# Third attention's reciprocals in long units, its normalisation two additions later, and five smaller moves in a four-layer network

## The reference

```
x += tanh(g0) * linear_attention(ln(x), ctx)      # L0_attn, feature maps Wqf, Wkf
x += tanh(g0') * ternary_ffn(ln(x))               # L0_ffn, 512 -> 2048 -> 512
x += tanh(g1) * masked_attention(ln(x), ctx)      # L1_attn, scores clipped to +-50, mask by key
x += tanh(g1') * product_key_experts(ln(x))       # L1_ffn, top 8 of 128 x 128 keys, 4 heads
x += tanh(g2) * attention_int8(ln(x), ctx)        # L2_attn, q and output weights and inputs quantised
x += tanh(g2') * moe(ln(x))                       # L2_ffn, 8 experts of 256, top 2
x += tanh(g3) * attention(ln(x), ctx)             # L3_attn
x += tanh(g3') * (shared + moe(ln(x)))            # L3_ffn, 8 experts of 352, top 2, shared 1408
attention: o = softmax(q k^T / sqrt(32)) v, per head, then o @ Wo + bo
```

## Time and profile before

| what | value |
| --- | --- |
| three runs | 3059.21, 3059.64, 3060.09 us; median 3059.64 |
| profiled execution, its own time | 3059.54 us |
| its span | 3057.8 us |
| mean granted TensorE clock | 0.932 of full speed |
| PE, DVE, ACT, POOL busy | 2632.1, 1753.8, 1196.7, 930.9 us |
| DMA | 333.52 MB |

### The profile page before, as it was taken

One profiled execution on the slowest core, in us unless ns is written; L12 is line 12 of the kernel. 1 busy time (PEld: TensorE's weight loads), 2 busy tenths in 40 slices (PEclk: granted clock), 3 DMA queues, 4 the chain that ended last, 5 costly groups with the idle time before them and its releaser, 6 DMA issues. The chain is left out here.

```text
span 3057.8 us, 36158 instructions
## 1 busy us (share of the span) xinstructions
PE 2632.1 (86%) x11447; PEld 1671.9 (55%) x11447; DVE 1753.8 (57%) x3263; ACT 1196.7 (39%) x2550; POOL 930.9 (30%) x434
## 2 busy tenths in 40 slices
PE   7998799788887679999959998738699998699898
PEld 3555487655434456656546553426476653477555
DVE  2444576467765989989377664512277773444221
ACT  0222222267743688788014555111125553222111
POOL 0222000066732110010015775033318982322122
PEclk9998899899988889999979999869899999799999
DMA  9663113665403410100063421074465430212722
GB/s 278 223 241 139 55 62 124 182 166 142 111 1 114 165 56 28 46 37 28 14 170 107 132 68 29 1 288 110 106 183 172 121 102 1 84 41 71 262 56 47
DMA packets 137548, 333.52 MB, mean 109 GB/s; under 512 B 18608, under 2 KB 21681, under 8 KB 133041
## 3 DMA queue, kind: packets, MB, share of 16 engines
q1 hardware_dynamic: 110192, 262.71, 27.7%
q0 software_dynamic: 12864, 29.06, 4.1%
q10 hardware_dynamic: 14336, 39.85, 3.9%
HBM read 237.24 MB, written 97.72 MB: 110 GB/s over the span
## 5 line engine op out<-in xcount | busy, mean ns | idle before, releaser
L1982 POOL TENSOR_TENSOR L_attn_total<-L_attn_total,L_attn_probs 128x2048 f32<-128x2048 f32 x103 | 471.8, 4581 | 31.6 <-ACT L_attn_probs L1910 22.1
L2016 DVE TENSOR_REDUCE L_attn_row_max<-L_attn_rows_ps 128x1 f32<-128x512 f32 x512 | 338.9, 684 | 149.6 <-PE L_attn_rows_ps L1776 145.5
L1910 ACT ACTIVATE L_attn_probs<-L_attn_s_ps 128x512 f32<-128x512 f32 x512 | 288.0, 601 | 269.1 <-PE L_attn_s_ps L1797 264.2
L521 PE MATMUL L_ffn_hidden<-L_ffn_x_high,L_ffn_up_high 128*128 128x512 f32 x688 | 295.9, 430 | 73.2 <-DVE L_ffn_routes L432 25.8
L1797 PE MATMUL L_attn_s_ps<-L_attn_q_stack,L_attn_k_stack 98*128 98x512 f32 (+1 forms) x768 | 311.7, 432 | 21.1 <-ACT L_attn_probs L1910 20.7
L398 ACT ACTIVATE L_ffn_sums<-sims 128x128 f32<-128x128 f32 x1024 | 314.5, 389 | 29.0 <-DVE L_ffn_routes L418 22.3
L521 PE MATMUL L_ffn_hidden<-L_ffn_x_low,L_ffn_up_high 128*128 128x512 f32 x688 | 272.8, 397 | 0.0
L1776 PE MATMUL L_attn_rows_ps<-L_attn_k_stack,L_attn_q_stack 96*128 96x512 f32 x512 | 223.1, 439 | 23.0 <-DVE L_attn_row_max L2016 17.1
L542 PE MATMUL L_ffn_y<-L_ffn_down_in,L_ffn_h 128*128 128x512 f32 x512 | 230.8, 596 | 1.9 <-DVE L_ffn_h L649 1.9
L1797 PEld LDWEIGHTS L_attn_s_ps<-L_attn_q_stack,L_attn_k_stack 98*128 98x128 f32 (+1 forms) x768 | 145.7, 194 | 158.1 <-ACT L_attn_probs L1910 73.3
L1910 ACT ACTIVATE L_attn_probs<-L_attn_s_ps,keep_mask 128x512 f32<-128x512 f32 x256 | 183.8, 783 | 82.8 <-DVE L_attn_s_ps L2028 82.4
(11 more groups left out here) (310 smaller groups left out, 4526.2 us busy)
## 6 DMA issues: line engine op xcount, KB each, us to landing
L_attn_k_stack<-k_parts SPq DMA_DIRECT2D x144, 256.0 KB, 4.8
L_attn_q_stack<-q_parts SPq DMA_DIRECT2D x72, 256.0 KB, 6.0
k_parts<-L_attn_stage SPq DMA_DIRECT2D x32, 512.0 KB, 2.8
L_attn_abs_in<-in_L_ffn_w SPq DMA_DIRECT2D x12, 1024.0 KB, 10.8
L_attn_kv_parts<-L_attn_part ACTq DMA_DIRECT2D x12, 1024.0 KB, 4.8
L_attn_ctx<-ctx_parts SPq DMA_DIRECT2D x24, 512.0 KB, 9.3
L_attn_wv<-L_attn_kv_parts SPq DMA_DIRECT2D x24, 512.0 KB, 7.1
q_parts<-L_attn_stage SPq DMA_DIRECT2D x24, 512.0 KB, 3.6
```

The lines of the kernel that those rows point to most:

```text
L521: last = nc.tensor.matmul(hidden_ps[0:m, b, side, :], w[:, i, e0:e0 + m], x_parts[xp][:, i, h * HALF:(h + 1) * HALF], start=(q == 0), stop ...
L1910: nc.scalar.activation(probs[:, g % P_SLOTS, h, :], s_ps[:, v % S_SLOTS, :], ACT.Exp, **kinds).then_inc(exp_done, 1)
L1982: nc.gpsimd.tensor_tensor(total[:], first, probs[:, g % P_SLOTS], ALU.add).then_inc(added, 1)
L2016: nc.vector.tensor_reduce(row_max[:, hq, i:i + 1], rows_ps[:, r % R_SLOTS, :], AX_X, ALU.max, negate=True).then_inc(max_done, 1)
```

## The change

Eight edits in one:

1. `linear_attention_block` loads wo and bo of L0 into its buffers for the value weights once these are used; the output block takes them from there.
2. The mask of L1 is loaded and made inside the attention block; `key_mask_block` goes.
3. `tile_stats.taken` is set again behind the guest work (`meanwhile`) in L1_ffn's block, so the L2 attention doesn't take the statistics a second time.
4. The L2 attention's opening order is another.
5. L2: the reciprocals are taken in eight parts of 64 columns at units 10, 10, 10, 14, 15, 16, 17, 17, where there were four of 128 at units 8 to 11.
6. L2: `normalise` stands behind addition kt = 5, not 3.
7. L2_ffn: two experts' weights are loaded in the norm block, and the other six in the routed block, once the scatter has landed.
8. The routed block no longer loads x back; the L3 attention does, at the head of SP's queue, and takes the statistics at S0 of its order, which is new too. In the other attentions S0 is first.

```diff
@@ def ffn_block(...), behind the call of meanwhile
+            env.tile_stats.taken = final
@@ def routed_block(...)
-    if not last:
-        env.tile_stats.begin(env)
             def _(sp):
+                sp.wait_ge(slots.scattered, 16 * PICKS * TILES)
                 sp.dma_start(sums.rearrange("(t p) d -> p t d", p=P), env.x[:]).then_inc(kept, 16)
                 load_weights(sp)
...
                 sp.wait_ge(summed, 16 * I)
-                if not last:
-                    for t in range(TILES):
-                        sp.dma_start(env.x[:, t, :], sums[t * P:(t + 1) * P, :]).then_inc(back[t], 16)
...
-                if not last:
-                    for t in range(TILES):
-                        dve.wait_ge(back[t], 16)
-                        env.tile_stats.take(env, dve, t)
-                    env.tile_stats.finish(dve)
@@ def streamed_attention_block(..., x_sums=None)
-    INVERT_AT = {u: part for part, u in enumerate((8, 9, 10, 11) if less_max_rows else (4, 6, 7, 8, 9, 10, 11, 12))}
-    INVERTED = SEQ // len(INVERT_AT)
-    NORM_KT = 3
+    invert_units = (10, 10, 10, 14, 15, 16, 17, 17) if made else (8, 9, 10, 11) if less_max_rows else (4, 6, 7, 8, 9, 10, 11, 12)
+    INVERT_PARTS = len(invert_units)
+    INVERT_AT = {u: [part for part, v in enumerate(invert_units) if v == u] for u in invert_units}
+    INVERTED = SEQ // INVERT_PARTS
+    NORM_KT = 5 if made else 3
...
     if made:
-        order = ("N0 X0 X1 N2 W0 W1 X2 X3 N4 Q00 V00 V01 X4 X5 W2 W3 N6 Q01 V02 V03 X6 X7 Q02 Q03 Q10 Q11 T0 Q12 Q13")
+        order = ("W0 W1 N0 N2 X0 X1 X2 X3 N4 Q00 W2 Q01 W3 V00 Q02 V01 N6 Q03 X4 X5 V02 X6 X7 V03 Q10 Q11 T0 Q12 Q13")
...
     else:
         order = ("N0 N1 K00 N2 N3 X0 X1 K01 N4 N5 X2 X3 W0 W1 V00 N6 N7 X4 X5 Q00 W2 W3 V01 X6 X7 Q01 K10 K11 "
                  "V02 V03 Q02 Q03 Q10 Q11 T0 Q12 Q13")
+    if x_sums is None:
+        order = "S0 " + order
+    else:
+        order = ("K00 K01 V00 V01 W0 W1 S0 N0 N1 V02 N2 N3 X0 X1 V03 N4 N5 X2 X3 Q00 W2 W3 N6 N7 X4 X5 Q01 X6 X7 K10 K11 "
+                 "Q02 Q03 Q10 Q11 T0 Q12 Q13")
...
+                if not less_max_rows:
+                    sp.dma_start(mask_raw[:], io["mask"]).then_inc(mask_loaded, 16)
+                if x_sums is not None:
+                    for t in range(TILES):
+                        sp.dma_start(env.x[:, t, :], x_sums[t * P:(t + 1) * P, :]).then_inc(x_back[t], 16)
                 parts.first_loads(env, sp)
...
+                def statistics():
+                    if not taken_before:
+                        for t in range(TILES):
+                            if x_sums is not None:
+                                dve.wait_ge(x_back[t], 16)
+                            nc.vector.bn_stats(stats[:, t, :], env.x[:, t, :]).then_inc(stats_done, 1)
...
@@ def linear_attention_block(..., wo_dram)
+                sp.wait_ge(v_done, CT)
+                sp.dma_start(wv[:], wo_dram).then_inc(env.wo_loaded, 16)
+                sp.dma_start(bv[:], io["bo"].partition_broadcast(P)).then_inc(env.wo_loaded, 16)
@@ def expert_layer(...), L2_ffn
+                    FIRST = 2
+                    def early(sp):
+                        slots.load_router(env, sp)
+                        for e in range(FIRST):
+                            load(sp, e)
+                    def rest(sp):
+                        for e in range(FIRST, EXPERTS):
+                            load(sp, e)
...
-                    routed_block(env, name, slots, (up_sb, down_sb), lambda sp: None, E, sums, last, ahead)
+                    routed_block(env, name, slots, (up_sb, down_sb), rest, E, sums, ahead)
```

More of the change, by code:

```diff
@@ L917, in _, with routed_block @@
                 dve.sem_inc(slots.placed, 1)
-def routed_block(env, name, slots, weights, load_weights, E, sums, last, ahead=None):
+def routed_block(env, name, slots, weights, load_weights, E, sums, ahead=None):
     nc = env.nc
@@ L1582, in streamed_attention_block @@
     env.wo_loaded = env.sem("wo_loaded")
+    x_back = [env.sem(f"x_back{t}") for t in range(TILES)] if x_sums is not None else []
     with ExitStack() as local:
@@ L1848, in _ @@
                         turn(0)
-                    elif item[0] not in "WN":
+                    elif item[0] not in "WNS":
                         for c in range(DC):
@@ L1936, in _ @@
                         high_turn(0)
+                if not less_max_rows:
+                    act.wait_ge(mask_step, 3)
                 for n in range(SETS):
@@ L2059, in quantised_pair @@
                     dve.sem_inc(xn_done, 2)
[L2061 to L2069, removed]
+                def statistics():
+                    if not taken_before:
+                        for t in range(TILES):
+                            if x_sums is not None:
+                                dve.wait_ge(x_back[t], 16)
+                            nc.vector.bn_stats(stats[:, t, :], env.x[:, t, :]).then_inc(stats_done, 1)
+                        for t in range(TILES):
+                            dve.wait_ge(stats_done, t + 1)
+                            nc.vector.bn_aggr(meanvar[:, t, :], stats[:, t, :]).then_inc(var_done, 1)
+                    dve.wait_ge(sd_done, 1)
+                    nc.vector.reciprocal(rstd[:], sd[:]).then_inc(rstd_done, 1)
+                    dve.wait_ge(rstd_done, 1)
+                if not less_max_rows:
+                    dve.wait_ge(mask_loaded, 16)
+                    keep = keep_mask[:, 1, :]
+                    nc.vector.tensor_scalar(keep, mask_raw[:], 0.5, None, ALU.is_gt).then_inc(mask_step, 1)
+                    dve.wait_ge(mask_step, 1)
+                    nc.vector.tensor_scalar(keep_mask[:, 0, :], keep, SCALE, None, ALU.mult).then_inc(mask_step, 1)
+                    dve.wait_ge(mask_step, 2)
+                    nc.vector.tensor_scalar(keep, keep, -1.0, BOUND, ALU.add, ALU.mult).then_inc(mask_step, 1)
                 for item in OPENING:
+                    if item[0] == "S":
+                        statistics()
                     if item[0] == "N":
@@ L2107, in _ @@
                         if u in INVERT_AT and n:
-                            invert(n - 1, INVERT_AT[u])
+                            for part in INVERT_AT[u]:
+                                invert(n - 1, part)
                         if less_max_rows and u == TURN_AT and n + 1 < SETS:
                             low_turn(n + 1)
-                for part in range(len(INVERT_AT)):
+                for part in range(INVERT_PARTS):
                     invert(SETS - 1, part)
@@ L2459, in _ @@
                 dve.wait_ge(abs_done, 3 * FG)
[L2462 to L2473, removed]
-                sp.dma_start(raw[:], io["mask"]).then_inc(loaded, 16)
-            @block.vector
-            def _(dve):
-                dve.wait_ge(loaded, 16)
-                nc.vector.tensor_scalar(keep[:], raw[:], 0.5, None, ALU.is_gt).then_inc(step, 1)
-                dve.wait_ge(step, 1)
-                nc.vector.tensor_scalar(keep_mask[:, 0, :], keep[:], 32 ** -0.5, None, ALU.mult).then_inc(step, 1)
-                nc.vector.tensor_scalar(keep_mask[:, 1, :], keep[:], -1.0, 50.0, ALU.add, ALU.mult).then_inc(step, 1)
-                dve.wait_ge(step, 3)
 def quantise_rows(nc, link, src, dst, top, tmp):
@@ L2521, in sb @@
             return local.enter_context(nc.sbuf_tensor(f"{name}_{n}", shape, dt))
-        if early:
+        if weights:
+            wo, bo = weights
+        elif early:
             wo, out_rows = env.out_weights[:, 0], env.out_weights[:, 1]
@@ L2758, in x_hat, with expert_layer @@
                 yield
-        def expert_layer(name, gate, shared, normalise, sums, last=False, ahead=None):
+        def expert_layer(name, gate, shared, normalise, sums, ahead=None):
             with sublayer() as local:
@@ L2886, in build @@
         if "L3_attn" in stages:
-            attention_layer("L3_attn", env.tanh_gates[:, 3:4], loads=loads3)
+            attention_layer("L3_attn", env.tanh_gates[:, 3:4], loads=loads3, x_sums=x_sums)
         between.close()
@@ L2890, in build @@
             expert_layer("L3_ffn", env.tanh_gates[:, 7:8], io["L3_ffn_shared_w1"].shape[0], False,
-                         out.rearrange("b s d -> (b s) d"), last=True)
+                         out.rearrange("b s d -> (b s) d"))
         else:
```

46 lines of the change are left out of this document (24 added, 22 removed).

## The result

The changed kernel takes 3097.31 us (median of four runs, 3095.62 to 3101.88) against 3059.43, a ratio of 1.0127 with a 95% interval of 1.0109 to 1.0145: some 39 us slower. The direction was forecast; both the forecast of 3075 and the upper end of the range, 3092, were too low.

The account below looks back on a forecast made before the run. TensorE, busy 86% of the span, was taken as the bound, so edits count by its idle time. Terms −5.5 −2.5 −0.2 −4 −13.5 +31 −1 +11 = +15.3 on 3059.6 gave 3075 us; range 3042 to 3092.

Parts of the forecast that it names:

- −5.5, −2.5, −0.2 and −4: Savings in us from L0's early output weights, L1's merged mask, L2's statistics not repeated, and L2's new opening order.
- The turn waits for the late normalisation: L2 attention: copies of the turn wait for GpSimd's normalise behind addition 5 in six sets, +31 us together.
- The cover of 2.1 us: L2 attention: of the turn's 6.3 us wait, 2.1 taken as covered by TensorE's other work, leaving 4.2 per set.
- The difference stays: L2 turn: if the faster front moves everything, additions too, by 3 us, normalise still ends 6.3 us after ScalarE is ready.
- The reciprocals: L2 attention: spread long units save 3.0 us in four sets, 1.5 in set 2, nothing in the last two: −13.5.
- +11 forecast: L3 attention opening with x reloaded inside: first row 11 us later; ends −6 and +14.
- −1 forecast: L2_ffn, experts' weights past the scatter: earlier block against contended xg loads, net −1 us, ends −4 and +3.
- The single contended wait: L2_ffn routed loop: one xg load in the weights' traffic makes TensorE wait, as 3.73 us in L3_ffn; about +4 once.
- rival (d): L2_ffn: late weights stall the routed loop more than once, +4 to the sum, 3079 us; inside the main case, together 0.48.
- (a): L2 turn's wait hides or is small (+3), reciprocals gain, L3 costs 11: 3047 us, or 3030 if L3 gains; chance 0.24.
- (b): Turn's wait as sized, but L3's opening gains 6 us: 3058, no change; chance 0.13.
- (c): Both costs, and stronger: turn's wait 5.5 us a set and half clock through each set's start, +45, 3089 us; chance 0.15.

## Why the prediction was right in direction and short in size

The parts, each by its own ratio x 3059: edits 1 and 2 +0.3, 3 and 4 +0.3, 5 and 6 +23, 7 +1, 8 +16; sum +40, measured +39. The forecast had −8, −4.2, +17.5, −1 and +11.

**Edits 1 to 4: the step that failed.** The forecast's −5.5, −2.5, −0.2 and −4, together −12.2, took every start that comes earlier as a gain of the total. The two runs of these edits measured 0 (−3 to +3) and 0 (−3 to +4). So half of the 24 us by which the forecast was short lies here. Each edit showed where it was to show (293.03, 543.07, Q00 at 1557.82), and then:

- Edit 1 kept about 4 of its 5.5 us.
- Edit 2 gave its 2.5 us back inside L1 (989.4 to 992.6 us from K00 on, against 985.4 to 989.2) and measured +5 alone. Why it costs more than its own opening shows stays open.
- Of the 4.2 us that edits 3 and 4 had gained at Q00, the stall behind N6, which grew from 4.42 to 5.56 us, and others left 2.2 at the first turn (76.1 us from the block's opening, 78.3 before).

The forecast never asked what is late next: the biases for the mask, the stall behind N6 for the order.

**The turn waits for the late normalisation: right, the term mis-sized.** "+31" for the six waits; edit 6 alone measured +36. Edits 5 and 6 with addition 5 against addition 4 are 32 us apart by their medians, 35 by the first transpose of the output in their traces, and addition 5 against 4 in the whole change 37. The cover of 2.1 us was right (in set 3 ScalarE's wait is 6.85 and TensorE's 4.92, 1.9 covered). The wait itself was 6.3 in the forecast and 6.2 measured with the old reciprocals; with the new ones it is 6.8 to 6.9 in five sets and 8.3 in the last. ScalarE then reaches the turn earlier, but GpSimd's additions don't move as far: in edit 6 alone GpSimd pauses 1.1 to 2.6 us for exponentials before addition kt = 4, and in the changed kernel it adds from kt = 1 to 5 without such a pause. "The difference stays" was thus wrong by 0.5 us in five sets and 2 in the last. The clock behind each wait was put at 1 us; in the set read of the changed kernel it costs 2.4 us (0.50 over 4.0 us, 0.80 over 1.9), and 3.4 in one of edit 6 alone (0.50 over 4.0, 0.66 over 4.0). This is the part of the term that was too small.

**The reciprocals: right in sum.** "−3.0 per set that has V chunks, −1.5 in set 2, nothing in the last two", −13.5: the periods give −1.2 and three times −2.8 where −3.0 stood, −4.3 in set 2 and 0, sum −13.9. That single sets are off is scatter of the trace of before, whose set 2 took 38.7 us where others took 35.9 to 37.4. The pieces take 521 ns, as near as the second attention's 537.

**Edit 8: the mechanism right, one term missing.** +11 forecast, +16 alone. From the opening of the block to the first row the forecast had 55 us and the trace 54. But the block was to open at "2197.4", 1.3 us after x is complete, and opens 5.0 after it. The row of the block's end says why: GpSimd drains its queue for 3.8 us once its last DMA has landed. Before, the same drain stood at 2196.2 and VectorE's statistics covered it. Moving them out exposed it, 3.7 us that the forecast took as gained. The bias loads were charged for the x loads' issue (3.65 us); they came 4.7 later, so 1 us was missing there too, and other terms gave it back.

**Edit 7: right within its ends when alone.** −1 forecast, +1 (−3 to +5) alone. The single contended wait was seen as priced, 4.6 us for 3.73. In the whole change the stage reads +5.1, above its upper end of +3: three later tiles waited longer there than in edit 7 alone (2.3, 1.4 and 3.0 us), as rival (d) had it. The changed kernel with addition 4, whose expert code is the same, has 2.6 us less from L2's output to the last xg, so this is at least in part scatter between executions, and no run tells more.

**Rivals.** (a) is refuted by the six waits. (b) is refuted in L3, where it wanted a gain of 6 us and under 40 us to the first row, and the runs show +16 and 54. (c), with both costs stronger than the main case, had the right direction in both, and its 3089 came nearest, but it named neither the failed early gains nor the drain.

## What to carry to other kernels

Before moving a slow engine's step later, look for what waits for its semaphore and who stands behind that waiter: here one number, 4 or 5, was worth 37 us, nearly the whole loss. When work is taken out of the end of a block, read what it had covered there; when a DMA is put ahead of small ones that a start waits for, charge it with its issue and its traffic. A start that comes earlier is a gain only if the next stage's last wait moves too.

## What the runs showed of the hardware

After its last indirect DMA had landed, GpSimd took 3.82 us to drain at the block's end (twice in every trace, 3818 and 3826 ns), while SP's drain took 0.007 to 0.12. TensorE's granted clock was 0.50 for 4 us behind a wait of 4.9 us, in the set that was read, and 1.00 again some 6 us behind it. In L1's opening TensorE is idle for 10.1 us ahead of K00 in the kernel before, and 9.4 with edit 1; the second window of 7 us from K00's start had a granted clock of 0.76 in the first and 1.00 in the second; why, no run shows.
